# Attention scores on Trainium2: per-head score tiles with mask matmuls, against 128x128 blocks of four heads with a mask written into a PSUM bank

## The reference, cut to what matters

```python
# x (8, 512, 256), 16 heads of 16 features each
k, q, v = proj(W_key), proj(W_query), proj(W_value)      # each (b, h, t, 16), times 256**-0.5
scores = einsum('bhqd,bhkd->bhqk', q, k) * 16 ** -0.5
scores = where(tril(ones((t, t))), scores, -inf)         # causal
weight = softmax(scores, axis=-1)
out = einsum('bhqk,bhkd->bhqd', weight, v)
out = out.transpose(0, 2, 1, 3).reshape(b, t, 256) @ W_proj * 256 ** -0.5
```

## Time and profile before

| | |
|---|---|
| median of three runs | 1073.25 us |
| profiled execution, its own time | 1071.2 us |
| its span | 1069.4 us |
| PE busy | 1008.3 us (94%), 6526 matmuls |
| ACT busy | 515.8 us (48%) |
| DVE busy | 499.9 us (47%) |
| POOL busy | 198.6 us (19%) |
| granted TensorE clock, mean over the span | 0.984 |

### The profile page before, as it was taken

The page is one execution under the profiler, slowest core; times in us unless marked ns, Lnnn a source line. Parts: engine busy times, 40 slices in busy tenths (PEclk is TensorE's granted clock), DMA queues, the critical chain, the costliest instruction groups (busy, mean ns, idle before and its releaser), DMA issues.

```text
span 1069.4 us, 20287 instructions
## 1 busy us (share of the span) xinstructions
PE 1008.3 (94%) x6526; PEld 684.7 (64%) x6526; DVE 499.9 (47%) x1147; ACT 515.8 (48%) x1384; POOL 198.6 (19%) x224
## 2 busy tenths in 40 slices
PE   6999999999999787899999999999999999999986
PEld 3677777777777653565665665665665666665653
DVE  5031123312121445565566566566566566566541
ACT  3344454444444422465465465465465465453433
POOL 5020111001000314204204204204204204200000
PEclk9999999999999987999999999999999999999999
DMA  8421112101003028052262263253253253225110
GB/s 250 150 71 67 59 49 69 40 31 59 29 29 128 20 99 177 22 173 55 71 190 56 70 186 60 69 185 61 69 182 64 69 178 68 70 85 104 32 40 20
DMA packets 66437, 93.75 MB, mean 88 GB/s; under 512 B 11872, under 2 KB 52832, under 8 KB 66400
## 3 DMA queue, kind: packets, MB, share of 16 engines
q1 hardware_dynamic: 60128, 88.83, 29.4%
q10 hardware_dynamic: 6272, 4.46, 1.3%
HBM read 59.41 MB, written 33.59 MB: 87 GB/s over the span
## 4 chain that ended last, share of the span: by engine, by line
PE 83%; DVE 6%; ACT 3%; issue 3%; DMA 1%; ACTq 1%; SPq 0%; POOL 0%; DVEq 0%; POOLq 0%
PE PS L843 26%; PE PS L1057 7%; PE PS L954 6%; PE PS L1006 6%; PE PS L1022 5%; PE PS L987 5%; PE PS L920 4%; PE PS L830 4%; PE PS L899 3%; PE PS L1088 3%; DVE nm L1740 3%; PE PS L941 2%; PE PS L1008 2%; PE PS L1044 2%; PE PS L1066 1%
## 5 line engine op out<-in xcount | busy, mean ns | idle before, releaser
L843 PE MATMUL PS<-arena 128*128 128x256 f32 x1024 | 313.7, 421 | 0.0
L1740 DVE TENSOR_REDUCE nm<-PS 128x1 f32<-128x512 f32 (+3 forms) x352 | 207.2, 636 | 89.9 <-PE PS L1008 89.8
L1390 ACT ACTIVATE arena<-PS 128x512 f32<-128x512 f32 x256 | 152.1, 600 | 169.8 <-PE PS L1044 169.7
L1251 ACT ACTIVATE arena<-PS 64x8 f32<-64x8 f32 x512 | 88.4, 173 | 184.9 <-PE PS L830 182.2
L830 PEld LDWEIGHTS PS<-arena 128*72 128x72 f32 x1024 | 128.8, 141 | 70.5 <-ACT arena L1251 7.3
L843 PEld LDWEIGHTS PS<-arena 128*128 128x128 f32 x1024 | 155.5, 192 | 0.0
L1022 PE MATMUL PS<-Q,K 98*128 98x512 bf16 (+3 forms) x512 | 120.4, 300 | 9.6 <-ACT arena L1390 5.1
L1590 DVE SCALAR_TENSOR_TENSOR arena<-arena 128x512 f32<-128x512 f32 x16 | 11.1, 694 | 249.1 <-ACT arena L1262 249.1
L830 PE MATMUL PS<-arena 128*72 128x8 f32 x1024 | 122.3, 192 | 0.0
L1006 PE MATMUL PS<-K,Q 96*128 96x256 bf16 (+3 forms) x512 | 112.9, 303 | 3.9 <-DMA K<-qk_d 1.8
L1008 PE MATMUL PS<-negmask,identb 128*128 128x128 bf16 (+2 forms) x352 | 86.8, 247 | 0.0
(11 more groups left out here) (189 smaller groups left out, 1293.1 us busy)
## 6 DMA issues: line engine op xcount, KB each, us to landing
qk_d<-QB SPq DMA_DIRECT2D x24, 512.0 KB, 3.0
Q<-qk_d SPq DMA_DIRECT2D x32, 192.0 KB, 3.9
K<-qk_d SPq DMA_DIRECT2D x32, 192.0 KB, 4.3
gt_d<-arena SPq DMA_DIRECT2D x16, 256.0 KB, 2.5
wx_d<-arena SPq DMA_DIRECT2D x16, 256.0 KB, 2.4
XT<-xt_d SPq DMA_DIRECT2D x8, 512.0 KB, 4.4
GT<-gt_d SPq DMA_DIRECT2D x8, 512.0 KB, 5.7
WX<-wx_d SPq DMA_DIRECT2D x8, 512.0 KB, 6.6
```

Source lines behind the costliest of these rows:

```text
L843: mm = pe.matmul(o, lhs, rhs, start=first, stop=last, skip_group_check=True)
L1390: s_.activation(PR[:, g % 2, j, at:at + T], PS[:, bank, :], ACT.Exp, scale=SCORE_SCALE).then_inc(t_e.sem, 1)
L1740: v_.tensor_reduce(nm[:, g, h:h + n, i], PS[:, u % 3, 0:n * (i + 1) * P].rearrange("p (n w) -> p n w", n=n), AX.X, ALU.max, negate=True).t ...
```

## The change: what it does

The ten units of a group become the ten 128x128 blocks (key tile, query tile) of the causal triangle, each for the four heads of the group side by side in one bank: 512 columns again, in four matmuls of 128 columns. Their order is `UNITS`. Four of them lie on the diagonal (`EDGES`, k = 0, 3, 6, 8). These go into bank 4 and accumulate (`start=False`) onto the mask that lies there; the six others go into bank 3. The mask matmuls are gone. Instead ScalarE, after the exponential of a diagonal unit and the side work of that step, waits for this exponential (`t_x`) and copies the mask from SBUF into bank 4 again (`write_edge`); the first mask is written by one matmul (`edge_bank`). A unit now waits for the last unit before it that has the same bank: for a diagonal unit, until the mask is written again; for another, until the exponential is taken. The exponential writes four pieces of 128 columns, one for each head, into `PR`, whose layout stays.

```diff
+UNITS = ((0, 0), (0, 1), (0, 2), (1, 1), (0, 3), (1, 2), (2, 2), (1, 3), (3, 3), (2, 3))
+EDGES = tuple(n for n, (kt, q) in enumerate(UNITS) if kt == q)
-TQ = 5 * GH // 2
+TQ = len(UNITS)
@@ TensorE
+            def edge_bank():
+                pe.wait_ge(c_w.sem, c_w.at(B, 0))
+                pe.matmul(PS[:, 4, :].rearrange("p (n w) -> p n w", n=GH), identb[:, :],
+                          negmask_t[:, :].unsqueeze(1).to_broadcast([P, GH, P]), start=True, stop=True)
             def turned(b, g, k):
                 if k == 0:
                     pe.wait_ge(m_ld[g].sem, m_ld[g].at(b, 2))
-                pe.wait_ge(t_e.sem, t_e.at(b, g * TQ + k - 1))
-                (the tiles of unit k, up to two turned_tile calls, into bank 3 + k % 2)
-                n = edge.shape[1]
-                pe.matmul(edge, identb[:, :], negmask_t[:, :].unsqueeze(1).to_broadcast([P, n, P]),
-                          start=False, stop=True).then_inc(t_mm.sem, 1)
+                kt, q = UNITS[k]
+                edge = kt == q
+                before = [n - TQ * (n >= k) for n in range(TQ) if (UNITS[n][0] == UNITS[n][1]) == edge]
+                pe.wait_ge(t_e.sem, t_e.at(b, g * TQ + max(before) + 1))
+                for j in range(GH):
+                    h = g * GH + j
+                    mm = pe.matmul(PS[:, 3 + edge, j * P:(j + 1) * P], K6[0:KM, h, kt * P:(kt + 1) * P],
+                                   Q6[0:KM, h, q * P:(q + 1) * P], start=not edge, stop=True,
+                                   skip_group_check=True)
+                mm.then_inc(t_mm.sem, 1)
@@ ScalarE
-                (exp of 512 columns of bank 3 + k % 2)
+                kt, q = UNITS[k]
+                at = P_AT[kt] + (q - kt) * P
+                bank = PS[:, 3 + (kt == q), :].rearrange("p (j q) -> p j q", q=P)
+                s_.activation(PR[:, g % 2, :, at:at + P], bank, ACT.Exp, scale=SCORE_SCALE
+                              ).then_inc((t_x if kt == q else t_e).sem, 1)
+            def write_edge(b, g, k):
+                act.wait_ge(t_x.sem, t_x.at(b, g * len(EDGES) + EDGES.index(k) + 1))
+                s_.copy(PS[:, 4, :].rearrange("p (j q) -> p j q", q=P),
+                        negmask_t[:, :].unsqueeze(1).to_broadcast([P, GH, P])).then_inc(t_e.sem, 1)
                 for k in range(TQ):
                     exp(b, g, k)
                     run(side, k)
+                    if k in EDGES:
+                        write_edge(b, g, k)
```

More of the change, by code:

```diff
@@ L34 @@
 P_AT = {0: 0, 1: 512, 3: 896, 2: 1024}
-PU = P_AT[2]
+UNITS = ((0, 0), (0, 1), (0, 2), (1, 1), (0, 3), (1, 2), (2, 2), (1, 3), (3, 3), (2, 3))
+EDGES = tuple(n for n, (kt, q) in enumerate(UNITS) if kt == q)
 G = 4
@@ L312, in two_layers @@
         t_e = count("t_e", TU, 2)
+        t_x = count("t_x", G * len(EDGES), 1)
         o_mm = count("o_mm", G, 2)
@@ L1183, in _ @@
             maxima_turn(0, 0)
+            edge_bank()
             pe.wait_ge(y_v.sem, y_v.at(1, 2))
@@ L1210, in _ @@
             s_ = nc.scalar
-            for s in (b_xt, b_ue, c_h, c_t, g_t, n_x2, n_xt, q_e, q_1, d_e, h_e, e_t, t_e, o_e, r_e, x_n, g_h, m_a, n_xn,
+            for s in (b_xt, b_ue, c_h, c_t, g_t, t_x, n_x2, n_xt, q_e, q_1, d_e, h_e, e_t, t_e, o_e, r_e, x_n, g_h, m_a, n_xn,
                       w_e):
```

## The result

The changed kernel takes 1100.62 us (median of 4 runs, 1099.81 to 1102.13). The kernel before took 1072.51 us in the runs beside it (4 runs, 1070.49 to 1073.43). The ratio is 1.0266 (95% interval 1.0247 to 1.0286): 28 us slower. The forecast was 1080 us with a range up to 1090, so the direction was right and the size far too small. The profiled execution's span is 1098.5 us against 1069.4, its mean granted clock 0.955 against 0.984.

The account below looks back on a forecast made before the run. TensorE, busy 94%, was taken as the bound on average, with ScalarE later at stage ends. 1071.2 us plus 3.5 for stalls net of savings plus 5.1 for clock falls gave 1079.8, forecast as 1080, range 1062 to 1090.

Parts of the forecast that it names:

- TensorE's part: TensorE, all ten units: four 128-column matmuls take 0.23 us, saving 0.80 us a stage, 25.6 us over 32 stages.
- rival (c): TensorE's small matmuls cost more in this stream: a unit takes 0.32 us instead of 0.23; 1092 us, chance 0.05.
- ScalarE's part: 128 mask copies on ScalarE, 0.60 us each, 0.67 until TensorE runs; most hidden, ACT busy up 70 to 80 us.
- the step on k = 6: Stage 3: the copy delays unit 7's exponential by 0.5 us, but DMA issues start before it and are not later.
- The copy behind k = 8: Not hidden, delays the next stage's unit 0 and values: 1.08 us lost at stage 3's end, 0.92 at stage 2's.
- What of the saving reaches the end: Only units where TensorE sets the time count: 0.55, 0.40, 0.45, 0.25 us kept in stages 0 to 3, 1.65 a sequence.
- The last sequence: Little side work there: the chain of exponentials, mask copies and waits starts the values 1.7 us later; together +1.6 us.
- the clock's: Behind stage 3's longer end wait the granted clock falls at three of seven places, 1.7 us each: 5.1 us.
- (a): Stalls cancel the gain, clock stays: 1074.7 us on the profiled execution, 1076.7 on the median; chance 0.25.
- (b): The saving reaches the end if mask copies land beside other waits or are much cheaper: 1062 us; chance 0.20.
- (d): The mask copy on ScalarE takes 1.04 us, the upper bound: 9 us more, 1089 us; chance 0.10.
- The row at 448 us: Clock evidence in the old trace: after 2.28 us of idleness between two full stretches the granted clock stayed at 1.00.

Follow-up runs that it names:

- experiment 4: The kernel before, without its mask matmuls on the transposed scores and with nothing in their place (scores unmasked, exponential's scale 0.02): 1062.32 us, 0.9899 of before.
- experiment 6: The changed kernel without the mask copy behind unit 8, the other three kept (unit 0 unmasked, exponential's scale 0.02): 1064.55 us, 0.9948 of before.
- experiment 2: The changed kernel with four idle matmuls at each stage 3 end and one ahead of the distance matmuls: 1076.06 us, 1.0054 of before.
- experiment 1: The changed kernel with four idle fp32 matmuls at each stage 3 end, before TensorE waits for the mask copy: 1080.21 us, 1.0089 of before.
- experiment 7: The changed kernel with all copies but reordered blocks, diagonal units at k = 1, 3, 6, 9, values not waiting for the last copy: 1063.62 us, 0.9951.
- experiment 5: Also called e4: the changed kernel with plain diagonal blocks and no mask copies (unmasked, exponential's scale 0.02): 1065.77 us, 0.9941 of before.
- experiment 3: The changed kernel with the mask copy behind unit 8 put ahead of that step's side work: 1082.54 us, 1.0123 of before.

## Why the prediction was wrong, by its steps

**TensorE's part was right.** A unit takes 0.23 us as forecast. By the rule of the Trainium skill (TensorE: Matmul & The Clock Gate, § Back-to-back issue gap), 81 ns a matmul, it would be 0.32; the trace disagrees, and rival (c) falls. (At 0.32 a stage would not have saved a few hundredths, as the prediction has it: 10 x 0.32 = 3.2 us against 4 x 0.28 + 6 x 0.33 = 3.1 is 0.1 us more.)

**ScalarE's part was right.** The copy was put at 0.60 us and takes 0.591; busy time rose by 66.9 us, a little under the 70 to 80. The release took 0.64 us (675.74 to 676.38) where 0.67 was taken. That three copies out of four are hidden holds: they cost 0.04 us a sequence, no more than the scatter (experiments 4 and 6). In stage 3 the DMA issue at 672.51 starts ahead of the exponential at 673.23, as the step on k = 6 had it.

**The copy behind k = 8 was right in place and price.** Forecast were waits of 2.4 and 1.2 us at the ends of stages 3 and 2; measured 2.09 and 1.01. The losses of 1.08 and 0.92 were to make 2.00 us a sequence; experiments 2 and 6 give 1.85.

**What of the saving reaches the end**: 1.65 us a sequence was forecast, 1.40 measured (80.6 - 79.20, experiment 6). With the 1.85 of the copies that makes +0.45 where the sum had +0.35.

**The last sequence** was to cost 1.6 us up to the last `values`. In experiment 2, which holds the clock ahead of it, these start 1055.38 - 991.78 = 63.60 us behind the last mark, where it was 61.28: 2.3. But inside the last sequence the clock falls there too, and further than before. Experiment 2 over ten of these us, where the kernel before has a clock of 0.83:

```profile
1020.00:1030.00 10.00, 7.84 (x57) 3.40 (x58) 2.16 (x4) 4.07 (x8) 0.00 (x0) 0.66 0.11 36
```

So no run shows how much of the 2.3 is the longer chain of waits, which the forecast meant, and how much is clock. One consequence was missed: the last `values` now fall on the lower clock and take 4.50 us instead of 2.36, another 2.1. The end of the changed kernel's timeline:

```profile
1080.70 4.50 PE L1052 MATMUL PS<-arena 128*32 128x512 f32 x32 [1.31 <-ACT arena L1382]
```

**The step that failed is the clock's: "I take three falls in the seven such places, 3 x 1.7 = 5.1 us".** Both factors were too small. Of the seven places, six show a fall, five of them a long one. And a fall doesn't cost the 1.7 us of one set of `values`: that number came from the end of the kernel, where the mean of 0.83 over the ten us from 1020 on makes 3.4 us at 0.50. Here it stays at 0.50 for six to seven us five times, over unit 0, three score steps, the `values` and the start of stage 0. A steady period is 85.4, the held one 81.05, so the clock takes 4.35 us of it; 1.45 of that is the short fall of experiment 1, which the prediction didn't have at all, and 2.9 the long one. With the clock held the six periods would take 991.78 - 507.22 = 484.6 instead of 505.6 us: 21.0 us of clock. The seventh place takes 65.30 - 63.60 = 1.7, the last `values` 2.1. Together about 25 us where 5.1 stood. The other terms come to 29.1 - 24.8 = 4.3 at most, against the forecast's 3.5; the fall at 467 us and those of the last sequence are still in them. Another way to the same: experiment 2's span is 1073.2 us, 25.3 less than the changed kernel's and 3.8 more than before, and in these 3.8 the 2.1 of the last `values` are clock again.

**The rivals.** (a), stalls alone with the clock as it was, is what experiment 2 runs: forecast 1076.7, measured 1076.06. That the totals meet is in part luck: experiment 2 lies 6.1 us above the kernel before in the runs beside it, where (a) had 3.5. (b), the faster side, was put on a cheap copy or another releaser; neither happened, but its mechanism is what experiment 7 makes true by taking the copy off unit 0's path: 1063.62, near (b)'s 1062. (d) falls with the 591 ns.

**The reading error.** The row at 448 us was read as evidence that a wait of this length might do no harm. That was not wrong in itself, as the first of the seven waits did none; but the row at 1020 us, with the same units and the same `values` behind it, was the nearer one, and the count of three falls came from neither. And the fall's length was taken over from a place where it was short, without a bound from above. Seven falls at 2.9 us alone would have put the sum at 1071.2 + 3.5 + 20.3 = 1095.

**What stays open.** Why the first of the seven waits (2.02 us) is followed by no fall, the seventh (2.12 us) by a short one, and the others by long ones; what ends a fall; and why the short fall behind `distance` comes in each sequence that had a long one, but only in some of the others: in five of seven in experiment 1, three in experiment 7, two each in experiments 5 and 6. The wait ahead of it is 0.51 to 0.54 us in the middle of all these kernels, with mask copies or without, against 0.30 before. The runs show that idle matmuls in the waits remove both falls, and that a unit 0 without a mask copy ahead of it removes the long one.

## What to carry to other kernels

A wait of one or two us on a TensorE that is busy 94% must be priced with the clock behind it: here the waits and the work cost 4 us at most and the clock 25. When a producer is moved off the bottleneck engine, ask first for its one deadline that lies behind other work, not for the load: three quarters of these copies cost nothing that could be measured, and one quarter, by its waits and the clock behind them, brought nearly all of the loss, and an order of the blocks that needed no copy at the seam turned +2.7% into -0.5%. If a wait can't be moved, idle matmuls in it give most of the loss back.

## What the runs showed of the hardware

- Waits at the end of stage 3, on a TensorE that was otherwise nearly always busy, were followed by a granted clock of 0.50 (1.2 GHz): those of 1.25 us (experiment 3) in seven cases of seven, six times for three to four us; those of 2.0 to 2.1 us (the changed kernel) in six of seven, five times for six to seven us. Waits of 0.35 us there (experiment 7) were followed by none.
- A fall has a price at the following work and not at the wait: a 512-column `values` matmul goes from 633 ns on average (experiment 2) to 795, and a unit's row from 0.40 to 0.61 us. A long fall cost 2.9 us of a period, a short one 1.45 (experiment 1) or 1.0 (experiments 6 and 7).
- Idle fp32 matmuls in a wait kept the granted clock at 1.00 behind it: 1100.62 to 1080.21 us with one place held, 1076.06 with two.
- Four matmuls of 128 columns with 98 rows and four different weights take 0.23 us in a stream, 57 ns each, in the kernel before, the changed one and e4.
- ScalarE's copy of 512 elements a partition from SBUF (bf16) into a PSUM bank (f32) takes 591 ns, a copy of as many out of PSUM 580. TensorE accumulates onto what ScalarE wrote into the bank: the diagonal units of the changed kernel and of experiment 7 get their mask in this way (but for the very first, which a matmul writes), and experiment 7 computes the whole reference.
